# Last layer's product as seven block products over pairs of neighbouring token tiles

## The chip, the cores and the metric

The kernel runs on one core of a Trainium2 chip. The metric is the device time of one execution in microseconds (us). TensorE (PE) multiplies, VectorE (DVE), ScalarE (ACT) and GpSimd (POOL) work on vectors, and SyncE (SP) issues every transfer of this kernel. Each of the five runs its own list of instructions in order and waits for others on semaphores.

## The reference, cut to what matters

Two layers run over 2048 tokens (4 batches of 512) of 1024 features. What the change rewrites is the last step, the second layer's feed-forward part, and what it moves stands behind the product before it, the attention's output projection:

```python
out = einsum('bhqk,bkhd->bqhd', attn, v).reshape(B, S, H * VD)
return out @ wo.T                       # added to x by the caller

# _L1_ffn_ref, with x = layernorm of the stream
q = x[:, Q_START:Q_END, :].mean(axis=1)
routing = softmax(q @ router_W.T + router_b)
base = x @ W.T + b                      # W: 1024 x 1024
t = einsum('bsd,erd->bser', x, A)       # 8 experts x rank 16 = 128 columns
lora = einsum('bser,eor,be->bso', t, B, routing) * SCALING
return base + lora                      # added to x by the caller
```

## The kernel before, in words

Tokens stand in 16 tiles of 128, resident in SBUF as `xb` (128 partitions x 16 x 1024, f32). Every matrix product of f32 data is made of f16 halves: a value is scaled and split into a high f16 part and a low f16 part, and `mm3` (lines 46 to 50) issues three products, high by high, high by low and low by high, into the same accumulator bank. So three matmuls stand for one in all that follows.

**Making the halves.** `Norm` (line 57) gives mean and reciprocal deviation of a tile: DVE statistics (`dve_stats`, lines 83, 84, 87), POOL for the power (`pool_rstd`, lines 92, 95), DVE for the normed rows (`dve_apply`, line 105). `Feed` (line 113) then takes the high half on ACT (`act_high`, line 174), the low half on POOL (`pool_low`, line 179), and SP turns both by a transposing DMA (`sp_turn`, line 186), so that features stand on partitions.

**Output projection** (`out_projection`, line 2192; names `E_...`). For each of 16 tiles `j`, 16 blocks of `kt` are multiplied in two banks of 512 columns, 96 matmuls a tile. The attention's output stands in DRAM (`od`); SP turns tile `j` into one of three buffers `ow_ot` (`ow.sp_turn(e, j)`, line 668), which it may do once tile `j - 3` is multiplied (the wait on `s_col`). DVE adds each finished tile to `xb` (`add(j)`, line 2246). PE may start tile `j` when `ow_ot` has landed and `add(j - 3)` has freed the banks. Between those, SP loads the last layer's weights and squares for their scale are made on ACT (`lw.act_square`); the totals are made behind tile 9 (`TOTALS`), and after that weights are scaled and split (`lw.act_split` on ACT, line 1308, `lw.dve_split` on DVE, line 1315) straight into SBUF: four parts here, ten more at the start of the last function. The first three tiles' rows are normed behind tiles 3, 4 and 5 (`NORMED`).

**Last layer** (`lora_layer1`, line 2323; names `F_...`). The 1160 columns (8 of the router, 128 of the adapters' first factor, 1024 of the base matrix) are cut in three chunks of 392, 384 and 384 (`CH`). For each tile `columns(t, c)` runs 8 blocks of `k` by three matmuls into bank `F_o`, 24 matmuls a chunk, 72 a tile. ACT keeps the router's and the adapters' columns (`keep`, lines 2454, 2455); DVE adds the rest to the stream (`finish`, line 2534); POOL adds the bias (`add_bias`, line 2566). Once a batch of four tiles is through, the router's mean and softmax (`router`, line 2392 on PE), the turned and routed adapter rows (`turn_w`, line 2398; `high_w`, `low_w`, lines 2445 and 2512), and the adapters' second product (`adapter`, six matmuls of 512 columns into `F_tr`, read by line 2521) are set into the middle of later chunks by the list `inside`. For the last batch they stand in and behind the last chunks (`ORDER`). A finished tile goes out in one transfer (line 2584).

The order on each engine is written out by hand; nothing is scheduled by a program. Between two functions stands a barrier of all engines (the branch at line 2314).

Of the kernel before, what the change touches and what calls it, by code (L numbers as in the profile page):

```python
# [17 lines left out]
NT = 16  # L18
# [211 lines left out]
def layers(nc, a, out):  # L230
    root = ExitStack()
    with root:
# [25 lines left out]
        g["ow"] = ow = OutWeights(nc, root, mwd, od, ms)  # L258
        mid, banks = ExitStack(), ExitStack()
# [7 lines left out]
        with ExitStack() as right:  # L267
            with ExitStack() as both:
# [9 lines left out]
                first(**g)  # L278
# [3 lines left out]
                lora_layer0(**g)  # L282
# [7 lines left out]
        with ExitStack() as outs, ExitStack() as last:  # L290
            ow.place(outs)
            ow.ob = bk + [outs.enter_context(nc.psum_tensor("bk3", [128, 512], F))] + qu.qb
            attention(**g)
            mid.close()
            feed.place(last, "N1", "left", 2 * NT, (1, 2, 0))
            feed.hT = [keep[:, 1024 * i:1024 * i + 1024].bitcast(H16).rearrange("p (k c) -> p k c", k=2 * KD) for i in range(3)]
            lw.place(lambda name, shape, dt=F: last.enter_context(nc.sbuf_tensor(f"F1_{name}", shape, dt)), a,
                     [r[:, 0:784] for r in ow.raw])
            out_projection(**g)
            outs.close()  # L300
            banks.close()
            lora_layer1(**g)


class Scope:


    def __init__(self, nc, name):
        self.nc, self.name, self.ctx = nc, name, ExitStack()
# [8 lines left out]
    def sem(self, name):  # L318
        return self.ctx.enter_context(self.nc.semaphore(f"{self.name}_{name}"))
# [289 lines left out]
class OutWeights:  # L609
# [61 lines left out]
    def pe_turned(self, w, j, kt):  # L671
# [3 lines left out]
        else:  # L675
            w.wait_ge(self.s_o[j % 3], 16 * self.G * (1 if j % 3 else 2) + 16 * (j // 3))


def first(nc, a, wbd, mwd, cst, vec, half, ident, xb, norm, msq, lnr, room, feed, lw, ones, s_c, bk, keep, bias, s_xb, **_):
# [443 lines left out]
    ph.ctx.close()  # L1123


class Lora:
# [12 lines left out]
    def place0(self, sb, a, room):  # L1139


        self.L, self.a, self.ring, self.had, self.again = 0, a, 6, [0] * 6, 0
# [18 lines left out]
    def place(self, sb, a, raw):  # L1161


        self.L, self.a, self.raw = 1, a, raw
        self.sb = sb
        self.ring, self.had, self.again = 3, [3, 3, 2], self.N
        self.W = [self.pair("w", 0)]
        self.junk = sb("junk", [128, 784], H16)
        self.small()
        self.w_v = a["w1"].rearrange("(k p) n -> p k n", p=128)  # L1170

# [5 lines left out]
    def pair(self, what, c):  # L1177
        return [self.sb(f"{what}{c}{x}", [128, KD, CH[c][1]], H16) for x in "hl"]

    def place_rest(self, sb):  # L1180
        self.sb = sb
        self.W += [self.pair("w", 1), self.pair("w", 2)]
        self.BT = [sb("bh", [128, D], H16), sb("bl", [128, D], H16)]

    def split_done(self, w, n):

        w.wait_ge(self.s_wl, self.N * self.L + n + 1)
# [4 lines left out]
    def inverses_done(self, w, n):  # L1192

        w.wait_ge(self.s_inv, 2 * self.L + (1 if n < 5 else 2))

    def scale_done(self, w, c):

        w.wait_ge(self.s_sc, 3 if self.L else 2 if c else 1)

    def slot(self, q):  # L1200

        i = q % self.ring
        return i, self.had[i] + q // self.ring + 1
# [11 lines left out]
    def source(self, q):  # L1215

        c = self.PARTS[q % self.N][0]
        wd = CH[c][1] if c < 3 else 256
        return self.raw[q % len(self.raw)][:, 0:2 * wd].rearrange("p (k n) -> p k n", k=2)
# [7 lines left out]
    def sp_load(self, e, w, q):  # L1227
        c, k = self.PARTS[q % self.N]
        p = q - self.ring
        if 0 <= p < self.again or not self.L:  # L1230
            w.wait_ge(self.s_sq, self.N * self.L + p + 1)
        elif p >= 0:
            self.split_done(w, p - self.again)
# [3 lines left out]
        else:  # L1237
            e.dma_start(self.source(q), self.a[f"B{self.L}"][:, 512 * k:512 * k + 512].rearrange("p (k n) -> p k n", k=2)
                        ).then_inc(self.s_raw[self.slot(q)[0]], 16)

    def act_square(self, e, w, n):
        src = self.source(n)
        self.landed(w, n)
        w.wait_ge(self.s_sq, self.N * self.L + n)
# [3 lines left out]
    def pe_totals(self, e, w, ones, bank, n0=0, n1=N):  # L1248
        w.wait_ge(self.s_sq, self.N * self.L + n1)
# [23 lines left out]
    def dve_totals(self, e, w, bank, s_tot):  # L1273

        w.wait_ge(self.s_sum, 3)
# [1411 lines left out]
```

## Time and profile before

| What | Value |
|---|---|
| Median of 3 runs | 1598.59 us (1597.6 to 1601.69) |
| Profiled execution, first to last instruction | 1596.5 us |
| Median less that span | 2.1 us |
| PE busy | 1539.0 us, 96% |
| DVE, ACT, POOL busy | 1030.4, 878.4, 806.3 us |

Busy time says how long an engine had an instruction in it. For PE the length of one matmul row is not its cost, since matmuls overlap; the distance from one start to the next is. The function called output projection ends its products near 1373 us, the last layer's run from 1375 to 1592.6 us.

### The profile page before, as it was taken

Reading aid. Unit: us, or ns where it says so; the run is one execution under the profiler, and the core shown is the slowest. Engines: PE = TensorE matmul, PEld = TensorE weight load, DVE = VectorE, ACT = ScalarE, POOL = GpSimd, SP = SyncE. Lnnn points to the kernel's source line nnn. Section 1 sums busy time; section 2 is a strip of 40 time slices with the busy share of each in tenths; the row PEclk is TensorE's granted clock in tenths of the full one; section 3 lists DMA queues with packets and bytes.
Section 4 is the critical chain, followed back from the end, with each engine's and each line's share of the span. In section 5 each row is a group of like instructions: output and inputs, shape, how many; then the busy total and the mean of one; then the engine's idle time right before and its main releaser. Section 6 shows DMA issues by size and latency. Waiting matters only on the chain. (4 is left out here: it accounts for less than half of the span.)

```text
span 1596.5 us, 32012 instructions
## 1 busy us (share of the span) xinstructions
PE 1539.0 (96%) x12384; PEld 948.8 (59%) x12384; DVE 1030.4 (65%) x2745; ACT 878.4 (55%) x1665; POOL 806.3 (51%) x706
## 2 busy tenths in 40 slices
PE   5998999999999999999999999999999999999998
PEld 4656555555556777677777777644444444566564
DVE  8898869986778888888888888742110100444433
ACT  6887324323769999999999999941110000211110
POOL 4223244446948888888888888820100000244450
PEclk9999999999999999999999999999999999999999
DMA  9994245545939999999999999988763330223331
GB/s 366 317 327 149 67 94 145 159 132 127 165 83 165 190 179 180 189 189 198 186 199 186 194 177 188 187 214 221 192 150 79 80 93 1 87 62 80 93 80 66
DMA packets 556503, 248.78 MB, mean 156 GB/s; under 512 B 498368, under 2 KB 531264, under 8 KB 556224
## 3 DMA queue, kind: packets, MB, share of 16 engines
q1 hardware_dynamic: 556352, 246.74, 67.1%
q8 instruction: 98, 1.61, 0.4%
q14 instruction: 53, 0.43, 0.1%
HBM read 73.68 MB, written 48.23 MB: 76 GB/s over the span
## 5 line engine op out<-in xcount | busy, mean ns | idle before, releaser
L2128 POOL TENSOR_TENSOR xb<-xb 128x1280 f16<-128x1280 f32 x128 | 335.7, 2623 | 5.3 <-ACT xb L2031 5.3
L2023 ACT ACTIVATE xb<-bk,D_sv,qw_c 128x512 f32<-128x512 f32 (+3 forms) x512 | 289.1, 622 | 2.4 <-DVE D_sv L2086 2.2
L2077 DVE TENSOR_REDUCE bk<-bk 128x1 f32<-128x512 f32 (+3 forms) x512 | 227.8, 491 | 15.9 <-PE bk L1973 15.2
L2031 ACT ACTIVATE xb<-xb 128x1280 f16<-128x1280 f32 x128 | 162.7, 1271 | 12.2 <-DMA xb<-xb 8.5
L92 POOL TENSOR_SCALAR mv<-mv 128x1 f32<-128x1 f32 x64 | 27.6, 431 | 279.4 <-DVE mv L87 278.3
L1988 PE MATMUL D_t<-vh,xb 128*128 128x65 f16 x1280 | 130.8, 194 | 1.6 <-DVE D_on L2096 1.6
L1989 PE MATMUL D_t<-vl,xb 128*128 128x65 f16 x1280 | 130.9, 192 | 0.0
L1990 PE MATMUL D_t<-vh,xb 128*128 128x65 f16 x1280 | 130.3, 193 | 0.0
L2246 DVE SCALAR_TENSOR_TENSOR xb<-bk,ms_c,xb 128x512 f32<-128x512 f32 x22 | 15.5, 746 | 166.0 <-PE bk L50 166.0
L1988 PEld LDWEIGHTS D_t<-vh,xb 128*128 128x128 f16 x1280 | 118.7, 97 | 2.5 <-issue 2.2
L1989 PEld LDWEIGHTS D_t<-vl,xb 128*128 128x128 f16 x1280 | 118.4, 98 | 0.4
L1990 PEld LDWEIGHTS D_t<-vh,xb 128*128 128x128 f16 x1280 | 118.6, 97 | 0.0
L2566 POOL TENSOR_TENSOR xb<-xb,F_bias 128x1024 f32<-128x1024 f32 x16 | 38.2, 2394 | 131.7 <-DMA F_mean<-in_cst 131.7
L2134 POOL TENSOR_TENSOR D_os<-D_on,D_os 128x256 f16<-128x256 f32 x128 | 87.6, 685 | 6.8 <-ACT D_os L2046 6.8
L606 POOL TENSOR_TENSOR D_qs<-D_qs,keep 128x256 f32<-128x256 f32 x84 | 61.1, 727 | 56.3 <-DVE keep L601 56.3
L174 ACT ACTIVATE N_hl<-N_h 128x1024 f16<-128x1024 f32 x26 | 27.4, 1054 | 108.9 <-DVE N_h L105 108.7
L48 PE MATMUL bk<-E_mh,ow_ot 128*128 128x512 f16 x220 | 83.4, 379 | 0.0
L49 PE MATMUL bk<-E_ml,ow_ot 128*128 128x512 f16 x220 | 83.4, 379 | 0.0
L50 PE MATMUL bk<-E_mh,ow_ot 128*128 128x512 f16 x220 | 83.4, 379 | 0.0
L566 PE MATMUL bk<-kTh,keep 128*128 128x512 f16 (+3 forms) x256 | 76.7, 299 | 2.7 <-DVE keep L551 1.3
L566 PE MATMUL bk<-kTh,D_QTh 128*128 128x512 f16 (+3 forms) x256 | 76.7, 299 | 1.3 <-ACT xb L2023 1.2
L567 PE MATMUL bk<-kTl,D_QTh 128*128 128x512 f16 (+3 forms) x256 | 76.6, 299 | 0.0
(367 smaller groups left out, 4627.5 us busy)
## 6 DMA issues: line engine op xcount, KB each, us to landing
od<-D_os SPq DMA_DIRECT2D x32, 512.0 KB, 4.6
xd<-xb SPq DMA_DIRECT2D x16, 512.0 KB, 4.0
ow_raw<-mwd SPq DMA_DIRECT2D x32, 256.0 KB, 3.4
xb<-xd SPq DMA_DIRECT2D x16, 512.0 KB, 5.9
out_x<-xb SPq DMA_DIRECT2D x16, 512.0 KB, 2.9
xb<-in_x SPq DMA_DIRECT2D x6, 1024.0 KB, 14.3
A_wo<-in_wo SPq DMA_DIRECT2D x6, 1024.0 KB, 6.8
ow_raw<-in_w SPq DMA_DIRECT2D x16, 384.0 KB, 4.6
```

Source lines behind the costliest of these rows:

```text
L48: e.matmul(out, a[0], b[0], start=start, stop=False, **kw)
L49: e.matmul(out, a[0], b[1], start=False, stop=False, **kw)
L50: return e.matmul(out, a[1], b[0], start=False, stop=stop, **kw)
L566: e.matmul(ps, qh, kT[0][:, k0:k0 + M], start=i > 0, stop=False)
L1988: e.matmul(o, pt[:, c, :], v[0][:, t, 0:65], start=j == 0, stop=False)
L1989: e.matmul(o, pt[:, c, :], v[1][:, t, 0:65], start=False, stop=False)
L1990: m = e.matmul(o, pt[:, 10 + c, :], v[0][:, t, 0:65], start=False, stop=j == i)
L2023: m = e.activation(p[:, AT[i]:AT[i] + N], Sb[n % 4][:, c:c + N], ACT.Exp, scale=qw.col(qw.NEG, g), bias=s[:, 7 - i:8 - i])
L2031: e.activation(P2[u % 3][:, 0:1280], P[u % 3][:, :], ACT.Copy).then_inc(s_ph, 1)
L2077: m = e.tensor_reduce(minima(u, i), Sb[n % 4][:, c:c + N], AX.X, ALU.min)
L2128: e.tensor_tensor(P2[u % 3][:, 1280:2560], P[u % 3][:, :], P2[u % 3][:, 0:1280], ALU.subtract).then_inc(s_pl, 1)
L2134: e.tensor_tensor(o[:, :, 1, 64 * h:64 * h + 64], on[u % 2][:, :, :], o[:, :, 0, 64 * h:64 * h + 64], ALU.subtract).then_inc(s_ol, 1)
```

## The change

**In the last layer** tiles are taken in pairs, 2p and 2p + 1. With the two tiles as rows of blocks, the two halves of the 1024 features as columns of blocks, and the base matrix in four blocks of 512 x 512, the product of a pair is made of seven block products (4 blocks of `k`, 512 columns each) where the plain way has eight. For this `PairFeed` makes two more tiles of rows a pair, sums and differences of halves (`dve_sums`, four DVE instructions of 512), each of which is split and turned like a tile. Of the seven blocks of weights three are blocks of the base matrix and four (`T1` to `T4`) are sums of such blocks. The seven products go into four banks (`X` twice, `Y`, `Z`), some on top of others; DVE reads a bank after each product (`read`, seven reads of 512 columns a pair, the running sum of a bank being what is read), and later products into that bank wait for the read (`read_before`). The 136 columns of router and adapters are a product of their own (`gates`, 48 matmuls of 136 columns a pair), made between product 5 and 6 of the pair before. The adapters' work stands at fixed places in odd pairs (`ODD`), the router's in even ones (`EVEN`). The last tile's halves go out apart.

**In the output projection** the rows and sums of pair 0 are made on DVE behind `add(1)` instead of tiles 0 to 2 behind 3 to 5; totals stand behind tile 6 instead of 9. The weights are then prepared in eight pieces (four blocks of `k` by two halves of the columns): POOL makes four sums a piece (`pool_sums`), ACT and DVE split the seven blocks' pieces (768 and 1024 columns), into one single buffer `O` that lies in the free tiles 12 to 15 of `xb`, and SP stores them to DRAM (`w1d`, two transfers a piece). The table `LOWS` says behind which tile's `add` DVE does this: pieces 0 to 2 behind tile 7, 3 to 5 behind tile 8, 6 and 7 with router, adapters and `B` behind tile 9. SP stores them in the turn of the loop that follows. The blocks are loaded back: one in turn 11, three as the last tile frees the output projection's first weight buffers (`ow.early`), three at the start of the last layer.

**Elsewhere** `Scope` gives its semaphores back; POOL clears the first function's at the start of `lora_layer0`.

```diff
+    PREPARED = [(j, c) for j in range(4) for c in range(2)]
+    ITEMS = PREPARED + [("g", 0), ("g", 1), ("b", 0)]
...
+    def stored_before(self, n):
+        return 32 * min(n, 8)
+
+    def act_high(self, e, w, n):
+        w.wait_ge(self.s_sc, 1)
+        self.landed(w, n)
+        if n < 8:
+            w.wait_ge(self.s_sums, 4 * n + 4)
+        w.wait_ge(self.s_out, self.stored_before(n))
+        parts = self.splits(n)
+        for i, (o, src, kind) in enumerate(parts):
+            x = e.activation(o[0], src, ACT.Copy, scale=self.scale(kind))
+        x.then_inc(self.s_hi, 1)
+
+    def dve_low(self, e, w, n):
+        w.wait_ge(self.s_sc, 1)
+        w.wait_ge(self.s_hi, n + 1)
+        for o, src, kind in self.splits(n):
+            i = e.scalar_tensor_tensor(o[1], src, self.scale(kind), o[0], ALU.mult, ALU.subtract)
+        i.then_inc(self.s_lo, 1)
+
+    def sp_store(self, e, w, n):
+        x, c = self.ITEMS[n]
+        w.wait_ge(self.s_lo, n + 1)
+        for l in range(2):
...
+                to, of = self.w1d[:, :, l, x, 256 * c:256 * c + 256].rearrange("b p n -> p b n"), self.O[:, l, :, :]
+            e.dma_start(to, of).then_inc(self.s_out, 16)
...
 def out_projection(...)
-    NORMED, TOTALS = 3, 9
+    TOTALS = 6
+    LOWS = {7: (0, 1, 2), 8: (3, 4, 5), 9: (6, 7, 8, 9, 10)}
...
         for j in range(NT):
             add(j)
-            if NORMED <= j < NORMED + 3:
-                stats(j - NORMED)
-                feed.dve_apply(e, w, N1 + j - NORMED, xb[:, j - NORMED, :])
+            if j == 1:
+                for q in range(2):
+                    stats(q)
+                    pf.dve_apply(e, w, q, xb)
+                for part in range(2):
+                    pf.dve_sums(e, w, 0, part)
...
+            for n in LOWS.get(j, ()):
+                lx.dve_low(e, w, n)
...
         for j in range(G, NT):
             w.wait_ge(s_col, j - 2)
             ow.sp_turn(e, j)
...
+            for n in LOWS.get(j - 1, ()):
+                if n < 8 or n == 10:
+                    lx.sp_store(e, w, n)
+                if n + 3 < len(lx.ITEMS):
+                    lx.sp_load(e, w, n + 3)
...
 def lora_layer1(...)
+    PRODUCTS = [("X", 0, 0, lx.B11), ("Z", 0, 4, lx.B21), ("X", 2, 4, lx.T2), ("Y", 3, 0, lx.T3), ("X", 2, 0, lx.T1),
+                ("Y", 1, 4, lx.T4), ("X", 3, 4, lx.B22)]
+    EVEN = {11: "r"}
+    ODD = {0: "w0", 2: "a0", 3: "w1", 5: "a1", 6: "w2", 8: "a2", 9: "w3", 11: "a3"}
...
+    def read_before(p, i):
+        return [7 * (p - 2) + 7, 7 * (p - 1) + 2, 7 * p + 1, 7 * (p - 1) + 6, 7 * p + 3, 7 * p + 4, 7 * p + 5][i]
...
+        gates(0)
+        for p in range(NP):
+            for s in range(14):
+                half_product(p, s // 2, s % 2)
+                x = inside(p, s)
+                if x:
+                    {"r": router, "w": turn_w, "a": adapter}[x[0]](x[1])
+                if s == 9 and p + 1 < NP:
+                    gates(p + 1)
```

How the instructions move is shown at two places. The first is SP's list from tile 7's turn on in the output projection, before (`E_col` is the count of finished tiles, `W_sq` that of squares, `ow_ot` the turned tile, `keep<-N1_hl` a normed tile being turned):

```order
L668 DMA_TRANSPOSE ow_ot2<-od 128x32x128 [waits E_col]
L1236 DMA ow_raw0<-in_w1 128x2x392 [waits W_sq]
L1236 DMA ow_raw1<-in_w1 128x2x384 [waits W_sq]
L1236 DMA ow_raw2<-in_w1 128x2x384 [waits W_sq]
L668 DMA_TRANSPOSE ow_ot0<-od 128x32x128 [waits E_col]
L186 DMA_TRANSPOSE keep<-N1_hl0 128x16x128 [waits N_lo]
```

and in the changed kernel from tile 8's turn to tile 9's (the count of finished tiles is here printed `A_mst0`, since the semaphore is reused; `X_lo` counts the pieces whose low halves DVE has made):

```order
L679 DMA_TRANSPOSE ow_ot2<-od 128x32x128 [waits A_mst0]
L868 DMA w1d<-xb 128x7x256 [waits X_lo]
L868 DMA w1d<-xb 128x7x256
L811 DMA ow_raw2<-in_w1 128x2x256 x2
L868 DMA w1d<-xb 128x7x256 [waits X_lo]
L868 DMA w1d<-xb 128x7x256
L811 DMA ow_raw0<-in_w1 128x2x256 x2
L868 DMA w1d<-xb 128x7x256 [waits X_lo]
L868 DMA w1d<-xb 128x7x256
L811 DMA ow_raw1<-in_w1 128x2x256 x2
L679 DMA_TRANSPOSE ow_ot0<-od 128x32x128 [waits A_mst0]
```

Before, SP waits only for finished tiles and for squares; now three waits for DVE's pieces stand between the turn of tile 8 and the turn of tile 9, and the same again between 9 and 10, and between 10 and 11. The second place is DVE's list there in the changed kernel (line 2507 is `add`, line 857 a low half, `X_hi` the count of pieces whose high halves ACT has made):

```order
L2507 SCALAR_TENSOR_TENSOR xb<-bk2,ms_c,xb 128x512 [waits A_mst0]
L2507 SCALAR_TENSOR_TENSOR xb<-bk3,ms_c,xb 128x512
L857 SCALAR_TENSOR_TENSOR xb<-ow_raw2,F1_sc,xb 128x768 [waits X_hi]
L857 SCALAR_TENSOR_TENSOR xb<-xb,F1_sc 128x1024
L857 SCALAR_TENSOR_TENSOR xb<-ow_raw0,F1_sc,xb 128x768 [waits X_hi]
L857 SCALAR_TENSOR_TENSOR xb<-xb,F1_sc 128x1024
L857 SCALAR_TENSOR_TENSOR xb<-ow_raw1,F1_sc,xb 128x768 [waits X_hi]
L857 SCALAR_TENSOR_TENSOR xb<-xb,F1_sc 128x1024
L2507 SCALAR_TENSOR_TENSOR xb<-qb0,ms_c,xb 128x512 [waits A_mst0,A_wo1]
L2507 SCALAR_TENSOR_TENSOR xb<-qb1,ms_c,xb 128x512
```

The three pieces stand between `add(7)` and `add(8)`; before, nothing stood there.

## Rows read from the trace of the kernel before

**Rows 1.** The page: granted clock of PE in 40 slices, in tenths.

```profile
PEclk9999999999999999999999999999999999999999
```

**Rows 2.** Windows: output projection's middle and the last layer (stretch, length, busy by engine).

```profile
1207.00:1269.00 62.00, 62.00 (x290) 28.28 (x289) 4.93 (x11) 2.62 (x3) 1.02 (x1) 1.00 0.34 85
...
1400.00:1575.00 175.00, 175.00 (x1060) 104.29 (x1058) 68.72 (x137) 23.60 (x56) 71.53 (x48) 1.00 0.29 73
```

**Rows 3.** Timeline of PE (start, length) at 1206 us: first and last of 13 starts.

```profile
1205.67 0.38 PE L48 MATMUL bk<-E_mh,ow_ot 128*128 128x512 f16 x1
...
1208.26 0.38 PE L48 MATMUL qb<-ow_mh,ow_ot 128*128 128x512 f16 x1
```

**Rows 4.** The same at 1040 us: first and last of 30 starts; the page's weight loads.

```profile
1040.15 0.19 PE L1988 MATMUL D_t<-vh,xb 128*128 128x65 f16 x1 [1.65 <-DVE D_on L2096]
...
1041.04 0.19 PE L1990 MATMUL D_t<-vh,xb 128*128 128x65 f16 x1
...
L1988 PEld LDWEIGHTS D_t<-vh,xb 128*128 128x128 f16 x1280 | 118.7, 97 | 2.5 <-issue 2.2
```

**Rows 5.** Groups by shape, the last layer: one of three and one of six.

```profile
L50 PE MATMUL F_o<-F_w0h,keep 128*128 128x392 f16 x128 | 42.1, 329 | 0.0
...
L48 PE MATMUL F_o<-F_w2h,keep 128*128 128x384 f16 x128 | 41.7, 326 | 0.0
```

**Rows 6.** Turns of attention output from 1165 to 1210 us: SP's time, then landing.

```profile
L668 SPq DMA_TRANSPOSE ow_ot<-od x3: 4674/4703/5277, 1165.7 to 1207.2; - x3
...
DMA to landing us min/median/max: 6.7/6.7/8.9
```

**Rows 7.** Timeline of DVE: the additions of tiles 7 and 8.

```profile
1207.17 1.41 DVE L2246 SCALAR_TENSOR_TENSOR xb<-bk,ms_c,xb 128x512 f32<-128x512 f32 x2 [17.87 <-PE bk L50]
1227.96 1.41 DVE L2246 SCALAR_TENSOR_TENSOR xb<-qb,ms_c,xb 128x512 f32<-128x512 f32 x2 [19.38 <-PE qb L50]
```

**Rows 8.** High and low halves by ACT and DVE: 1024 columns, then 768 and 784.

```profile
L655 ACT ACTIVATE E_mh<-ow_raw,ms_c x10: 1147/1148/1149, 1060.5 to 1081.6; 128x1024 f16<-128x1024 f32 x10
...
L659 DVE SCALAR_TENSOR_TENSOR E_ml<-ow_raw,ms_c,E_mh x10: 1283/1284/1286, 1061.7 to 1082.8; 128x1024 f16<-128x1024 f32 x10
...
L1308 ACT ACTIVATE F_w2h<-ow_raw,F_sc 128x768 f16<-128x768 f32 x4 | 3.6, 931 | 3.0 <-DMA ow_raw<-in_w 3.0
...
L1315 DVE SCALAR_TENSOR_TENSOR F_w0l<-ow_raw,F_sc,F_w0h 128x784 f16<-128x784 f32 x3 | 2.9, 1026 | 0.0
```

**Rows 9.** Stores to DRAM: SP's time and landing, 510 to 700 us; the page's median.

```profile
L2160 SPq DMA_DIRECT2D od<-D_os x11: 431/575/643, 515.2 to 697.1; - x11
...
DMA to landing us min/median/max: 3.2/4.0/7.4
...
od<-D_os SPq DMA_DIRECT2D x32, 512.0 KB, 4.6
```

**Rows 10.** Windows of PE's one long pause and what followed.

```profile
136.00:137.00 1.00, 0.00 (x0) 0.00 (x0) 1.00 (x2) 1.00 (x3) 1.00 (x2) 1.00 0.00 0
...
138.00:139.00 1.00, 1.00 (x6) 0.49 (x4) 1.00 (x3) 0.42 (x2) 0.00 (x0) 0.50 0.46 168
...
141.00:142.00 1.00, 1.00 (x5) 0.88 (x5) 0.00 (x0) 1.00 (x4) 0.00 (x0) 0.95 0.24 92
```

**Rows 11.** Groups by shape, last layer: POOL; then DVE beside POOL's work.

```profile
L2566 POOL TENSOR_TENSOR xb<-xb,F_bias 128x1024 f32<-128x1024 f32 x16 | 38.2, 2394 | 131.7 <-DMA F_mean<-in_cst 131.7
L179 POOL TENSOR_TENSOR N_hl<-N_h,N_hl 128x1024 f16<-128x1024 f32 x13 | 28.4, 2184 | 13.4 <-ACT N_hl L174 13.4
...
L1315 DVE SCALAR_TENSOR_TENSOR F_w2l<-ow_raw,F_sc,F_w2h 128x768 f16<-128x768 f32 x4 | 7.0, 1794 | 3.1 <-ACT F_w2h L1308 3.1
```

**Rows 12.** The page: a normed tile being turned; then a POOL timeline row at 149 us.

```profile
keep<-N_hl SPq DMA_TRANSPOSE x16, 4.3
...
149.37 0.89 POOL L92 TENSOR_SCALAR mv<-mv 128x1 f32<-128x1 f32 x1 [9.16 <-DVE mv L87]
```

**Rows 13.** Timeline of DVE: the end.

```profile
1592.03 1.41 DVE L2521 SCALAR_TENSOR_TENSOR xb<-F_tr,F_sc,xb 128x512 f32<-128x512 f32 x2 [0.99 <-PE F_tr L50]
```

More of the change, by code:

```diff
@@ L294, in layers @@
             mid.close()
[L295 to L298, printed above, removed]
+            lx.place(lambda name, shape, dt=F: last.enter_context(nc.sbuf_tensor(f"F1_{name}", shape, dt)), ow, xb)
+            pf.place(lambda name, shape, dt=F: last.enter_context(nc.sbuf_tensor(f"P_{name}", shape, dt)), keep, xb)
             out_projection(**g)
@@ L1175, in small @@
         self.sc = self.sb("sc", [128, 20])
[L1177 to L1183, printed above, removed]
     def split_done(self, w, n):
-        w.wait_ge(self.s_wl, self.N * self.L + n + 1)
+        w.wait_ge(self.s_wl, n + 1)
     def all_split(self, w):
@@ L1303, in act_split @@
         c = self.PARTS[n][0]
-        self.landed(w, self.again + n)
+        self.landed(w, n)
         self.scale_done(w, c)
-        if c and not self.L:
+        if c:
             self.split_done(w, 4 * c - 1)
-        e.activation(self.halves(n)[0], self.source(self.again + n), ACT.Copy, scale=self.scale(c)).then_inc(self.s_wh, 1)
+        e.activation(self.halves(n)[0], self.source(n), ACT.Copy, scale=self.scale(c)).then_inc(self.s_wh, 1)
     def dve_split(self, e, w, n):
@@ L2426, in pe, with gates @@
-        for x in ORDER:
-            if x[0] == "c":
-                columns(x[1], x[2])
-            else:
-                small(x)
+        def gates(p):
+            for i in range(2):
+                hi, lo = pf.halves(4 * p + i)
+                pf.turned(w, 4 * p + i)
+                w.wait_ge(s_ta, 2 * p)
+                for k in range(KD):
+                    x = mm3(e, gb[:, GN * i:GN * i + GN], (hi[:, k, :], lo[:, k, :]), (lx.G[0][:, k, :], lx.G[1][:, k, :]),
+                            k == 0, k == KD - 1)
+                x.then_inc(s_g, 1)
@@ new lines, in half_product @@
+        def half_product(p, i, h):
+            _, kind, k0, blk = PRODUCTS[i]
+            hi, lo = pf.halves(4 * p + kind)
+            W = lx.pe_block(w, blk)
+            pf.turned(w, 4 * p + kind)
+            w.wait_ge(s_fin, read_before(p, i))
+            for k in range(2 * h, 2 * h + 2):
+                x = mm3(e, bank(p, i)[:, :], (hi[:, k0 + k, :], lo[:, k0 + k, :]), (W[0][:, k, :], W[1][:, k, :]),
+                        k == 0 and i in (0, 1, 3), k == 3, skip_group_check=i in (2, 4, 5, 6))
+            if h:
+                x.then_inc(s_p, 1)
@@ L2592, in sp, with store @@
-        for t in range(2, NT):
-            if t + 2 < NT:
-                feed.sp_turn(e, w, N1 + t + 2)
-            for c in range(3):
-                for y in inner(t, c):
-                    if y[0] == "a":
-                        store(y[1])
-        for t in (12, 14, 15):
-            store(t)
-        w.wait_ge(s_out, 16 * NT)
+        def store(q, halves=(0, 1)):
+            t = pf.tile(q)
+            for c in halves:
+                e.dma_start(out[128 * t:128 * t + 128, 512 * c:512 * c + 512], xb[:, t, 512 * c:512 * c + 512]).then_inc(s_out, 16)
```

661 lines of the change are left out of this document (414 added, 247 removed).

## The prediction, made before the changed kernel was run

> **What bounds the kernel now.** I read the page first, then the windows, the groups by shape and the timelines of the two stages that the change touches. The clock row shows PE at its upper level, 2.4 GHz, in all 40 slices [rows 1]. The windows show PE busy for 62.00 of 62 us in the middle of the output projection and 175.00 of 175 in the last layer, with DVE at 4.93 and 68.72 and POOL at 1.02 and 71.53 us there [rows 2]. So in both stages the end is set by how many columns PE streams, as long as nobody keeps it waiting; a column saved is time saved, and a wait added to PE is time added in full. The output projection gives one tile in 20.7 us (96 matmuls at the distance below; DVE's additions of tiles 7 and 8 start 20.79 us apart, [rows 7]).
>
> **What a matmul costs** is the distance between two starts. For 512 columns, 12 distances take 1208.26 - 1205.67 = 2.59 us, so 215.8 ns each, or 0.4215 ns a column [rows 3]. For 65 columns, 29 distances take 0.89 us, so 30.7 ns each, each with a weight load of its own [rows 4].
>
> **The last layer, PE.** Before: three groups of 128 matmuls of 392 columns and six of 384 [rows 5], so 16 x 24 x 1160 = 445,440 columns. After, a pair takes 7 products x 4 blocks x 3 = 84 matmuls of 512 columns and 48 of 136: 49,536 columns, in all 396,288. The difference is 49,152 columns x 0.4215 ns = **20.7 us less**. Adapters, turns and routers are the same instructions elsewhere in the order. A gate matmul is thereby priced at 136 x 0.4215 = 57 ns. The row of 65 columns lies at 30.7 ns, 3.3 above its columns, so a weight load does not bind at 57 [rows 4]. *The Trainium skill (TensorE: Matmul & The Clock Gate, Back-to-back issue gap) says that in a stream of load and matmul pairs N = 128 takes some 81 ns; by it 384 gate matmuls would cost 9 us more. The trace does not agree: the distance of the 65-column pairs is well under that.*
>
> **The last layer, waits.** DVE and POOL get more work. POOL has, a pair, four low halves, two biases and two powers: 4 x 2.18 + 2 x 2.39 [rows 11] + 2 x 1.3 (an estimate: 0.89 in [rows 12] and a power of about half a us behind it) = 16 us, against PE's 20.9 us in an even pair (49,536 columns) and 27 in an odd one (24 adapter matmuls x 0.2158 and four turns more). The chain norm, high, low, turn (4.3 us, [rows 12]), then the sum rows through the same two buffers, biases and powers comes to 21 or 22 us: it fits, with little over in even pairs. DVE's low halves took 1794 ns beside POOL's work where 784 columns alone took 1026 [rows 8, 11]; the new sums have, like those, two inputs in SBUF, so I take them at double, some 1.3 us each instead of 0.7. In odd pairs the statistics and a late adapter read stand before the bank that the fourth turn needs: about 1 us a pair, 4 us in all. At the start, bias transfer and first bias of POOL end about 9 us in while product 3 wants the first bank read at 8 us: 1.7 us. Sum of waits **+5.7 us**; bounds 1 us (DVE always in time) and 16 us (each even pair stretched by 4 us on top if the chain is 25 us). I take the first because the chain's rows fit.
>
> **The end.** Before, two adapter reads of DVE start at 1592.03 [rows 13], the second on the bank that PE ends last, and a transfer of 512 KB ends at 1596.5. After, one read follows the last product, and 256 KB go out. I put half of one read on it: **-0.4 us**.
>
> **The output projection.** PE's matmuls stay the same. What changes is who releases them. Call the time at which tile 7 is multiplied 0; the next tile ends at 20.7. DVE then adds tile 7 (1.4 us, [rows 7]) and makes three pieces. There is one buffer `O`: the high half of piece n + 1 waits until both transfers of piece n have landed. So the round trip is store, high, low, in series:
> - store: the second transfer is issued 0.57 us after the first and lands 4.6 us later [rows 9]: 5.2 us. A piece has 448 KB in each of its two transfers, in runs of 512 bytes; the row has 512 KB in one. Bounds: 0.4 + 3.2 = 3.6 and 0.6 + 7.4 = 8.0 us [rows 9].
> - high, 768 and 1024 columns on ACT: 0.93 + 1.15 = 2.1 us [rows 8].
> - low on DVE: 0.98 + 1.28 = 2.25 us (the row for 784 columns scaled) [rows 8].
>
> Round trip c = 9.5 us, between 7.9 and 12.3. The first piece's high half is ready in time (totals stand behind tile 6, a tile earlier), so the lows end at 3.65, 3.65 + c and 3.65 + 2c. Behind the third wait SP issues two stores and two loads (2 us) and only then turns tile 9, which lands 6.7 us later [rows 6]: 12.35 + 2c = 31.4 us. PE wants it at 20.7 us. **Wait at tile 9: 2c - 8.35 = 10.7 us.** This wait did not exist: before, the same turn was issued when tile 6 had ended, a whole tile and more ahead.
>
> The next three pieces follow the same beat, the turn of tile 10 lands at 12.35 + 5c; PE wants it at 33.05 + 2c. **Wait at tile 10: 3c - 20.7 = 7.8 us.** Pieces 6 and 7 end 2c later, the rest takes a store of 5.2 us and 3.8 us of halves (544, 544 and 1024 columns), issue and landing 7.5 us: the turn of tile 11 lands at 20.15 + 7c, PE wants it at 33.05 + 5c. **Wait at tile 11: 2c - 12.9 = 6.1 us.** Together 7c - 42 = **+24.6 us**, between 13 and 44. For turn 12 nothing is left to wait for, and DVE's delayed additions cost nothing, because PE needs `add(8)` only for tile 11.
>
> **The clock.** PE stood still for the whole of 136 to 137 us; at 138 to 139 the granted clock was 0.50, the 1.2 GHz level, and in 141 to 142 it was 0.95, back again [rows 10]. Some 3.4 us at half speed lose 1.7 us. The waits above are longer. Three times 1.7 is **+5.1 us**; bounds 0 and 8 (the longest wait followed by twice as much).
>
> **The rest.** The first rows are made from 1100 us on, when DVE has 16 us and more between tiles; squares and totals end before they are wanted; loads of the first four blocks have the last five tiles for themselves; the three at the start of the last layer (1 MB each) are wanted from 13 us on, and the first lands about 8 us in. All at 0; if a block came late it would be by 1 to 2 us. POOL's clearing of 38 semaphores falls in a stretch in which it then waited 9.16 us for DVE [rows 12]: 0, at most 1 us.
>
> **Sum**: 24.6 + 5.1 - 20.7 + 5.7 - 0.4 = **+14.3 us**. The profiled execution of 1596.5 us and 2.1 us around it are just the median of 1598.6 us, so the forecast is **1612.9 us**. A measurement of this kernel can tell about 0.3%, 4.8 us, from no change: faster is below 1593.8, slower above 1603.4.
>
> **Rivals.**
> - *The round trip is short and the saved columns win.* Place: the store between two highs. With c = 7.9 the waits are 13.3 us, the last wait in the clock is small, say two drops, 3.4; with waits of 3 us in the last layer: 13.3 + 3.4 - 20.7 + 3 - 0.4 = -1.4, 1597 us, no change. To be faster c must be under 7.3 us, which needs a store of 2.9 us, below the shortest of [rows 9], unless stores are quicker here than in those rows, which stand beside the attention's own transfers. At c = 6.8: 5.4 for tile 9, then nearly nothing for 10, and 1 for 11: 6.4 + 2 - 20.7 + 3 - 0.4 = -9.7, **1589 us**. Against it: ACT and DVE alone take 4.35 of it. Chance of c that short 0.11, of the middle 0.13.
> - *The last layer is bound by its feed.* DVE's sums and POOL hold each other up, and the chain of an even pair takes 25 us instead of 21 or 22: four even pairs, some 10 us more, **1623 us**. For it: the 1794 ns of [rows 11]; against it: POOL's 16 us of work. Chance 0.12.
> - *Gate matmuls are bound by loading weights.* A load row is 97 ns long [rows 4]; if 384 gates took that instead of 57, 15 us more, **1628 us**; by the page's 81 ns it would be 9 us more. The 30.7 ns speak against it. Chance 0.03.
> - *The waits are there, but the change of products is not what saves*: if the seven products' bank order stalls PE at each product by the read (0.7 us and 0.3 us of delay against a product of 2.6 us), 56 x 0.3 = 17 us more. Each read has a whole product's time, so chance 0.01.
>
> **How the numbers follow.** The forecast, slower by 5 to 25 us, gets 0.60. Faster: 0.11 of the first rival and a little for errors that I don't see, 0.13. No change: 0.13, and the lower edge of the forecast, 0.02, is 0.15. Slower: 0.72. The range leaves out the fastest and the slowest tenth: from 1594 (c of 7.5) to 1630 (c of 11, or the feed on top).
>
> **What would show it.** Tile 9, 10 and 11 of the output projection start 11, 8 and 6 us late, each released by a turn (DMA on `ow_ot`), and the clock falls behind them. SP's longest waits are on DVE's low halves; ACT's highs wait for the stores (`w1d`). From store to the next high 5 us. The last layer's PE time is 197 us of work in a stretch of about 203. If PE has no pause at tile 9, the account of the output projection is wrong; if the last layer takes over 207 us, that of its feed is.

## The result, and the profile after

| | before | after |
|---|---|---|
| median of the runs, us | 1598.09 (1595.74 to 1601.69, 4 runs) | 1614.72 (1612.97 to 1617.57, 4 runs) |
| ratio to before, 95% interval | | 1.0104 (1.0087 to 1.0121) |
| profiled span, us | 1596.5 | 1614.9 |
| add of tile 7 to add of tile 15 | 165.9 us | 192.4 us |
| add of tile 15 to the end | 223.4 us | 212.3 us |

The change makes the kernel 1.0% slower: 1614.7 us against a forecast of 1612.9 us. The last layer became 11.1 us shorter, and the output projection in front of it 26.5 us longer. Of the 18.4 us between the two profiled spans, 3.0 lie ahead of tile 7's add (1210.18 against 1207.17 us). The nine kernels of the experiments run the changed kernel's code up to there and make this add at 1206.2 to 1209.7 us, so most of the 3.0 is the spread of single executions; the medians differ by 16.6. One of the four executions of the first experiment's kernel took 4651 us, with its granted clock at 1.00 and for a reason that nothing here shows; its median of 1591.01 us includes it, and the other three have a median of 1589.54.

The page of the changed kernel, with PE's share and the clock that answers to [rows 1]:

```profile
PE 1527.1 (95%) x12288; PEld 925.7 (57%) x12288; DVE 1095.9 (68%) x2791; ACT 899.0 (56%) x1680; POOL 858.8 (53%) x754
...
PEclk9999999999999999999999999999998999999999
```

One slice of the clock row, at three quarters of the span, now reads 8. All of PE's waits from 1085 us to the end (line, what it waited for: us in total, times, longest):

```profile
PE bk L48 <- DMA ow_ot<-od: 17.5, 2, 12.9
PE F_tr L2674 <- DVE xb L2788: 5.5, 9, 0.9
PE qb L48 <- DMA ow_ot<-od: 3.9, 1, 3.9
PE F_X L48 <- DVE xb L2799: 3.1, 4, 2.4
PE F_g L48 <- DMA F_hT<-P_hl: 2.3, 2, 1.8
PE F_g L48 <- PEq L2595: 1.8, 1, 1.8
```

Three waits for turns of the attention output come first, 21.4 us together. Where [rows 2] showed PE busy for 62.00 of 62 us, these are the first matmuls of tiles 9, 10 and 11 in PE's timeline (start, length, and in brackets the wait and its releaser):

```profile
1243.79 0.59 PE L48 MATMUL bk<-ow_mh,ow_ot 128*128 128x512 f16 x1 [12.93 <-DMA ow_ot<-od]
...
1271.75 0.58 PE L48 MATMUL bk<-ow_mh,ow_ot 128*128 128x512 f16 x1 [4.55 <-DMA ow_ot<-od]
...
1298.76 0.38 PE L48 MATMUL qb<-ow_mh,ow_ot 128*128 128x512 f16 x1 [3.93 <-DMA ow_ot<-od]
```

Why each turn is late stands in SP's timeline of the same stretch (start, time on the queue, transfer, count). Two stores, two loads, and only then the turn:

```profile
1232.53 0.97 SPq L868 DMA_DIRECT2D w1d<-xb  x2
1233.54 2.40 SPq L811 DMA_DIRECT2D ow_raw<-in_w  x2
1235.98 5.68 SPq L679 DMA_TRANSPOSE ow_ot<-od  x1
```

From the turn's issue to PE's start it is 1243.79 - 1235.98 = 7.8 us. What SP waits for is DVE's low half of a piece, and these follow at a steady beat. The low halves in DVE's timeline; ACT's high half releases them:

```profile
1211.50 1.01 DVE L857 SCALAR_TENSOR_TENSOR xb<-ow_raw,F_sc,xb 128x768 f16<-128x768 f32 x1
...
1220.92 1.02 DVE L857 SCALAR_TENSOR_TENSOR xb<-ow_raw,F_sc,xb 128x768 f16<-128x768 f32 x1 [7.21 <-ACT xb L850]
...
1230.28 1.02 DVE L857 SCALAR_TENSOR_TENSOR xb<-ow_raw,F_sc,xb 128x768 f16<-128x768 f32 x1 [7.15 <-ACT xb L850]
```

The beat is 9.4 us; the first and the sixth piece start 1258.41 - 1211.50 = 46.9 us apart, 9.38 each. And the clock, in windows of PE (stretch, length, busy PE, PEld, DVE, ACT, POOL, granted clock, DMA share, GB/s):

```profile
1234.00:1242.00 8.00, 0.00 (x0) 0.00 (x0) 2.21 (x2) 1.97 (x2) 1.45 (x3) 0.58 1.05 257
1242.00:1246.00 4.00, 2.21 (x6) 0.87 (x7) 0.00 (x0) 0.00 (x0) 2.81 (x4) 0.50 1.08 280
...
1270.00:1274.00 4.00, 2.25 (x6) 0.87 (x7) 0.77 (x1) 0.00 (x0) 0.00 (x0) 0.50 0.87 226
```

PE came out of its 12.93 us wait at the 1.2 GHz level, and from its first matmul to its add tile 9 took 1267.24 - 1243.79 = 23.4 us instead of 20.7.

That slow tile reaches the chain of pieces at one place. In DVE's list piece 6 stands behind tile 9's add, and the add waited for PE:

```profile
1267.24 1.41 DVE L2507 SCALAR_TENSOR_TENSOR xb<-bk,ms_c,xb 128x512 f32<-128x512 f32 x2 [6.62 <-PE bk L50]
1268.56 1.01 DVE L857 SCALAR_TENSOR_TENSOR xb<-ow_raw,F_sc,xb 128x768 f16<-128x768 f32 x1
```

The sixth low half had begun at 1258.41, so this one comes 10.2 us behind it instead of 9.4.

In the last layer, the new sums of DVE (groups by shape from 1402 us on: busy us, mean ns):

```profile
L935 DVE TENSOR_TENSOR ow_raw<-ow_raw 128x512 f32<-128x512 f32 x7 | 13.9, 1986 | 0.0
L936 DVE TENSOR_TENSOR F_s<-ow_raw 128x512 f32<-128x512 f32 x7 | 12.5, 1782 | 0.0
L941 DVE TENSOR_TENSOR F_s<-ow_raw 128x512 f32<-128x512 f32 x7 | 10.3, 1466 | 0.2
L939 DVE TENSOR_TENSOR ow_raw<-ow_raw 128x512 f32<-128x512 f32 x7 | 6.0, 859 | 0.0
```

The gate matmuls went as the columns say, not as their weight loads do. The first and third in PE's timeline:

```profile
1404.29 0.22 PE L48 MATMUL F_g<-F_gh,keep 128*128 128x136 f16 x1 [1.77 <-PEq L2595]
...
1404.41 0.22 PE L50 MATMUL F_g<-F_gh,keep 128*128 128x136 f16 x1
```

Two distances are 0.12 us: 60 ns each for 136 columns, where 57 had been put down.

### The profile page after: what moved, and what is told of

Read it like the earlier page. It is cut to its first block and busy times, and to the rows that moved or that the text cites. A ratio compares the mean times of both kernels' runs of the same rounds, so it can differ in the third digit from the quotient of the medians.

```text
span 1614.9 us, 32082 instructions
## 1 busy us (share of the span) xinstructions
PE 1527.1 (95%) x12288; PEld 925.7 (57%) x12288; DVE 1095.9 (68%) x2791; ACT 899.0 (56%) x1680; POOL 858.8 (53%) x754
## 5 line engine op out<-in xcount | busy, mean ns | idle before, releaser
L92 POOL TENSOR_SCALAR mv<-mv 128x1 f32<-128x1 f32 x64 | 22.1, 346 | 147.5 <-DVE mv L87 146.5
L2739 ACT ACTIVATE F_lg<-F_g,F_sc 128x8 f32<-128x8 f32 x16 | 4.3, 269 | 133.3 <-PE F_g L50 133.3
```

## The experiments

Theory A: the loss is SP's order. The turns of tiles 9 to 12 stand in one queue behind stores that wait for a 9.4 us round trip. The saving is real, and part of it is lost again in the last layer to sums of DVE. Rivals: the turns are late because DMA is busy, wherever they stand; the clock's fall is a cost of its own; each of the three waits is a fixed price; the last layer's waits follow from DVE's amount of work.

**The turns ahead of the stores.** The turns of tiles 9, 10 and 11 are issued ahead of the stores of pieces 0, 3 and 6, in place of behind the whole group of stores that such a piece begins, and tile 12's ahead of the last store (item 10, `B`).

```diff
+        AHEAD = {0: 9, 3: 10, 6: 11, 8: 12}
...
         for j in range(G, NT):
-            w.wait_ge(s_col, j - 2)
-            ow.sp_turn(e, j)
+            if j not in AHEAD.values():
+                turn(j)
...
+                if n in AHEAD:
+                    turn(AHEAD[n])
```

> SP's list alone is changed: the turn of tiles 9, 10, 11 and 12 is issued ahead of the stores of pieces 0, 3, 6 and 10, as soon as its own condition holds (tile j - 3 multiplied). DVE's, ACT's and POOL's lists and the single buffer O stay. Theory A (the cost in the output projection is the queue position of the turns behind the round trips of O): PE waits for no turn, the clock does not fall there, the round trip stays 9.4 us. Output projection 21.4 + 5.1 = 26.5 us shorter, total about 1588 us, some 10 us below the kernel before. Rival B (the added transfers themselves slow the turns, or DVE's low halves delay the additions that PE needs): the waits move to the additions or the turns still land late; total stays above 1605 us.

Measured: 1591.01 us, ratio 0.9945 (0.9925 to 0.9964) to the kernel before. PE's waits for turns are down from 21.4 to 0.5 us:

```profile
PE qb L48 <- DMA ow_ot<-od: 0.5, 1, 0.5
```

Tile 7 to tile 15 is 166.4 us, as before the change. The whole loss of the output projection hangs on these few places in SP's list; the same transfers still ran beside it. With its turns there the change makes the kernel 0.55% faster. The same kernel was run again:

> The kernel with the four turns ahead of the stores once more, as the base of this batch: 1591.0, within 1.5 us, ratio 0.9945 to the kernel before; last layer 213 us.

Measured: 1590.29 us, ratio 0.9947 (0.9934 to 0.996); add of tile 15 to the end 212.1 us.

**Only the turn of tile 9 ahead** (`AHEAD = {0: 9}`).

> Only the turn of tile 9 goes ahead of the stores. Theory A: the round trips go on at their own beat and the turns of tiles 10 and 11 are still behind them, so the wait at tile 9 vanishes and nearly all of it comes back at tile 10: 12.35 + 5c against 41.4 us with c = 9.4 gives 18 us there instead of 4.6, then 4 to 6 us at tile 11. Total within 4 us of the changed kernel, about 1612 us. Rival C (each block of three pieces costs its own wait, independent of the others): 12.9 us and one fall of the clock, 2.7 us, are saved, total about 1599 us.

Measured: 1612.84 us, ratio 1.0086 (1.0069 to 1.0103). The wait at tile 9 is gone and stands at tile 10:

```profile
PE bk L48 <- DMA ow_ot<-od: 20.1, 1, 20.1
...
PE qb L48 <- DMA ow_ot<-od: 0.7, 1, 0.7
```

So the three waits are not three prices. The time at which a turn behind the stores can land is set by the number of pieces ahead of it, and PE waits for it in one part or in three.

**The pauses filled.** PE runs 56, 20 and 16 matmuls into the bank `tot`, whose contents nobody reads again, ahead of tiles 9, 10 and 11, to stand still less: 4.4 us of waits for turns are left of 21.4. They are added work; nothing is left out.

```diff
+        FILL = {9: 56, 10: 20, 11: 16}
...
+            if j in FILL:
+                w.wait_ge(lx.s_inv, 2)
+                for n in range(FILL[j]):
+                    e.matmul(tot[:, :], ow.m(0, 15)[:, 0:128], ow.m(0, 15)[:, 0:512], start=True, stop=True)
```

> The changed kernel, with 56, 20 and 16 matmuls of 512 columns on data of no use issued ahead of tiles 9, 10 and 11, which end about when the turns land (12.1, 4.3 and 3.5 us of work against waits of 12.9, 4.6 and 3.9); they write a bank that nobody reads after. If the clock is what makes tiles 9 and 10 take 23.4 and 23.1 us instead of 20.7 (theory A), it stays at 2.4 GHz and the total is 5 us less, about 1610 us. If those tiles are slow for another reason (stores, loads and PE's reads in each other's way, rival D), they stay at 23 us and the total does not fall, 1615 us or a little more.

Measured: 1615.04 us, ratio 1.0097 (1.008 to 1.0114). At tile 9 the clock stayed up:

```profile
1234.00:1242.00 8.00, 6.55 (x32) 2.78 (x30) 2.21 (x2) 1.97 (x2) 2.81 (x4) 1.00 1.09 261
1242.00:1246.00 4.00, 4.00 (x20) 1.83 (x19) 0.10 (x1) 1.97 (x2) 0.00 (x0) 1.00 0.72 206
```

At tile 10 it did not. After a wait of 2.96 us PE came back at the upper level and fell to the lower one 1.1 us later (two of its rows at 1269.7 and 1270.2 us, matmuls 0.22 and then 0.43 us apart):

```profile
1269.71 0.38 PE L49 MATMUL bk<-ow_ml,ow_ot 128*128 128x512 f16 x1
...
1270.21 0.63 PE L48 MATMUL bk<-ow_mh,ow_ot 128*128 128x512 f16 x1
```

Tile 9 took 20.9 us instead of 23.4, tile 10 22.6 instead of 23.1. So PE's tiles got 3.0 us shorter, and hardly anything of it arrived: from tile 7's add to tile 11's start it is 88.2 us against 88.6, and tile 7 to tile 15 is 192.0 us against 192.4. Part of that is the fill's own doing: the turn of tile 11 landed at 1293.9 (issued at 1286.96, 6.9 us to landing), and PE was still filling until tile 11 began at 1294.70. Without this 0.8 us some 1.2 of the 3.0 us would have arrived. The expected gain of 5 us was a miss, and it shows the flaw in my account of the clock. The next turn lands when SP's beat lets it; a slow tile mostly uses up the wait that comes after it.

**The beat shortened.** On the changed kernel, turns behind the stores as in it: each piece's high half is stored as soon as ACT has made it, and only the low half waits for DVE.

```diff
-        w.wait_ge(self.s_lo, n + 1)
         for l in range(2):
+            w.wait_ge(self.s_hi if l == 0 else self.s_lo, n + 1)
```

> Base: the changed kernel itself, turns behind the stores as in it. Each piece's high half is stored as soon as ScalarE has made it, not when VectorE has made the low half as well, so that the round trip (beat c of the pieces, 9.4 us in the changed kernel) gets shorter. Theory A (the waits at tiles 9 to 11 add up to 7 beats less a fixed 42 us): c falls by about 0.9 us (VectorE's low half of 0.9 us and one issue of 0.5 us come off, if the second store's landing doesn't take their place), the wait of ow_ot from 21.4 us to about 15 us, T7 to T15 from 192.4 to about 186 us, total about 1608. If the second store's landing ends the beat as before: c falls by 0 to 0.5 us, total 1611 to 1615. Rival B (the three waits are each a turn's own landing, whatever the beat): waits and total as in the changed kernel, 1614.7, also with a shorter beat.

Measured: 1608.10 us, ratio 1.0062 (1.005 to 1.0074), 6.6 us under the changed kernel. The beat between low halves that follow each other without a turn fell to 7.6 us:

```profile
1209.57 1.01 DVE L857 SCALAR_TENSOR_TENSOR xb<-ow_raw,F_sc,xb 128x768 f16<-128x768 f32 x1
...
1217.12 1.02 DVE L857 SCALAR_TENSOR_TENSOR xb<-ow_raw,F_sc,xb 128x768 f16<-128x768 f32 x1 [5.34 <-ACT xb L850]
...
1232.29 1.02 DVE L857 SCALAR_TENSOR_TENSOR xb<-ow_raw,F_sc,xb 128x768 f16<-128x768 f32 x1 [1.85 <-ACT xb L850]
1241.81 1.02 DVE L857 SCALAR_TENSOR_TENSOR xb<-ow_raw,F_sc,xb 128x768 f16<-128x768 f32 x1 [7.31 <-ACT xb L850]
```

That is 1.8 us shorter, twice what I had expected, but the beat across a turn is 9.5 us (the last two rows): the next high half's store now comes while SP is still busy with the turn. From the first low half to the eighth it is 58.2 us where it was 68.0, so 8.3 us a beat. PE's waits for turns fell from 21.4 to 13.5 us, and tile 7 to tile 15 from 192.4 to 183.6 us. A shorter beat shortens the total, as the formula of the prediction has it: with c = 8.31 it gives 16.2 us, and tile 11 starts 77.4 us after tile 7's add against 62.1 before, 15.3 us late. Three fixed prices would have left it.

**The sums copied.** On the kernel with the turns ahead: the sums of pairs 1 to 7 are replaced by copies with one input, of the same size and at the same place. Left out are these sums.

```diff
-        if part == 0:
+        if p and part == 0:
...
+            e.tensor_scalar(sa[:, lo], h2[:, lo], 1.0, None, ALU.mult).then_inc(self.s_sum, 1)
+            e.tensor_scalar(sb[:, lo], h1[:, lo], 1.0, None, ALU.mult).then_inc(self.s_sum, 1)
...
```

> On top of e1_turn_first. In pairs 1 to 7 the four sums of rows a pair are replaced by plain scaled copies of one input, so the output leaves out the sums; number, width and place of the instructions are the same, but each reads one SBUF operand instead of two. Theory E (DVE's two-input sums are held up by POOL's instructions, 2 to 2.6 us instead of 0.7, and that makes bank reads and adapter reads late): the copies take 0.4 to 0.7 us each, PE's waits in the last layer fall from about 10 us to 4 or less, total about 6 us below e1_turn_first. Rival F (the waits come from the places of the adapters' work in the order, and would be there with any DVE work in between): the waits stay near 9 us and the total within 2 us of e1_turn_first.

Measured: 1586.82 us, ratio 0.9921 (0.9905 to 0.9938), last layer 207.7 us, 5.5 less than its base in the same batch. But the copies were held up too, if less (the page's groups, busy us and mean ns):

```profile
L935 DVE TENSOR_SCALAR ow_raw<-ow_raw 128x512 f32<-128x512 f32 x7 | 12.1, 1722 | 0.0
L936 DVE TENSOR_SCALAR F_s<-ow_raw 128x512 f32<-128x512 f32 x7 | 10.6, 1518 | 0.0
L939 DVE TENSOR_SCALAR F_s<-ow_raw 128x512 f32<-128x512 f32 x7 | 8.7, 1245 | 0.0
L938 DVE TENSOR_SCALAR ow_raw<-ow_raw 128x512 f32<-128x512 f32 x7 | 4.2, 595 | 0.0
```

I had expected 0.4 to 0.7 us each, which one of the four keeps to. PE's listed waits in the last layer fell from 11.9 us to 9.1, not to 4: those on DVE from 8.6 to 4.2, while the one on `F_hT` grew from 1.5 to 3.1. So the last layer does hang on how long DVE's four instructions take, some 0.25 us a sum here, but one input in place of two is no way out.

**The sums elsewhere.** The same sums, later in DVE's list: in steps 2 and 5 of pairs 1, 3 and 5, behind the reads that free PE's banks, and in steps 5 and 7 of pair 0; in pairs 2, 4 and 6 they keep their places. The statistics of odd pairs move from step 7 to step 9 with them.

```diff
+        SUMS_AT = [(5, 7)] + [(2, 5) if p % 2 else (1, 3) for p in range(1, NP)]
...
-                if p + 1 < NP and s in (1, 3):
-                    pf.dve_sums(e, w, p + 1, s // 2)
-                if p + 2 < NP and s == 7:
+                if p + 1 < NP and s in SUMS_AT[p]:
+                    pf.dve_sums(e, w, p + 1, SUMS_AT[p].index(s))
+                if p + 2 < NP and s == (9 if p % 2 else 7):
```

> Base: the kernel with the four turns ahead of the stores. Only the places of VectorE's sums move: for a pair that follows an odd pair they come after the adapter's product has been read and after the next pair's product (steps 2 and 5 in place of 1 and 3), the first pair's at steps 5 and 7. Theory A (the waits of F_tr and F_X in the last layer are there because a sum of VectorE, held up beside POOL by up to 2 us, stands ahead of the subtraction that frees the product's bank): those two waits fall from 8.6 us to about 3 us together, last layer about 208.5 us from the add of tile 15 to the end in place of 213.2, total 4 to 5 us below the base, about 1586.5. Rival B (VectorE is late by its whole amount of work, wherever the sums stand): the waits only move to other products, total within 1.5 us of the base, about 1591.

Measured: 1582.63 us, ratio 0.9905 (0.9892 to 0.9918), 7.7 us under its base in the same batch. The waits of `F_tr` and `F_X` on DVE fell from 8.7 to 0.7 us:

```profile
PE F_g L48 <- DMA F_hT<-P_hl: 4.0, 2, 3.6
PE F_g L48 <- PEq L2603: 1.8, 1, 1.8
...
PE F_X L48 <- DVE xb L2807: 0.7, 3, 0.2
```

The sums that moved also came to lie where POOL stands idle. DVE in pair 3, in the kernel with the turns ahead, with POOL's low half (line 962) that the first sum runs into (line 2796 is the read of the adapters' bank `F_tr`):

```profile
1461.23 2.13 POOL L962 TENSOR_TENSOR P_hl<-ow_raw,P_hl 128x1024 f16<-128x1024 f32 x1 [3.75 <-ACT P_hl L957]
...
1461.87 2.03 DVE L935 TENSOR_TENSOR ow_raw<-ow_raw 128x512 f32<-128x512 f32 x1
...
1464.43 1.40 DVE L2796 SCALAR_TENSOR_TENSOR xb<-F_tr,F_sc,xb 128x512 f32<-128x512 f32 x2
...
1467.57 2.50 DVE L941 TENSOR_TENSOR F_s<-ow_raw 128x512 f32<-128x512 f32 x1
```

and in this one:

```profile
1462.05 1.41 DVE L2796 SCALAR_TENSOR_TENSOR xb<-F_tr,F_sc,xb 128x512 f32<-128x512 f32 x2 [1.19 <-PE F_tr L50]
1463.37 0.68 DVE L935 TENSOR_TENSOR ow_raw<-ow_raw 128x512 f32<-128x512 f32 x1
...
1469.52 0.69 DVE L941 TENSOR_TENSOR F_s<-ow_raw 128x512 f32<-128x512 f32 x1
```

So the sums now stand behind the read of `F_tr`, and they are no longer held up: two of four took 2.03 and 2.50 us beside POOL, and all four take 0.68 or 0.69 with POOL idle. Over pairs 1 to 7 DVE's sums fell from 42.7 to 30.1 us in all. The run can't say which of the two took PE's waits away, and with less work of DVE it doesn't refute rival B cleanly either. The pairs that kept their places show that long sums alone need not cost much: their first two still take 1.99 and 2.61 us, and PE waits 0.24 us for `F_X` there, before and after. Add of tile 15 to the end is 205.4 us. What is left is new: the second pair's gates wait 3.6 us for the turn of their rows.

**The start of the last layer, ACT and POOL.** Rows 4 and 5 made ahead of other work there.

```diff
+        pf.act_high(e, w, 4)
         keep(0)
         keep(1)
...
+        pf.pool_low(e, w, 4)
         add_bias(0)
+        pf.pool_low(e, w, 5)
         add_bias(1)
...
```

> Base: the kernel with the sums later. At the last layer's start the high and the low half of row 4 and POOL's first halves are made ahead of the copies for the gates' second turn. Theory A (the gates of the second pair wait 1.5 to 3 us for their rows' second turn because of what stands ahead of it on ScalarE and POOL): these waits on F_hT and the one on the sequencer fall from 3.3 us to below 1.5 us, total 1 to 2 us below the base, about 1585. Rival B (the wait is for keep, which now comes later): the wait moves there and the total is the base's or up to 1 us above, 1587.

Measured: 1582.10 us, ratio 0.9898 (0.9885 to 0.9911), which can't be told from its base. The wait stayed at 4.1 us, so it was not what stands ahead of it on ACT and POOL. SP's timeline showed where it came from: row 4's low half was made at 1380.3, its turn issued behind the last of ten loads,

```profile
1376.07 0.33 SPq L2863 DMA_DIRECT2D F_bias<-in_b  x1
...
1380.06 0.57 SPq L877 DMA_DIRECT2D F_w3h<-w1d  x1
...
1384.90 0.48 SPq L2869 DMA_DIRECT2D F_bl<-b1d  x1
1385.43 19.61 SPq L966 DMA_TRANSPOSE F_hT<-P_hl  x4
```

and the gates were released at 1395.8, 10.4 us after that.

**The start of the last layer, SP.** The turns of rows 4 and 5 between the loads of the weights, which are wanted later.

```diff
         pf.sp_turn(e, w, 3)
-        for i in range(4, 7):
-            lx.sp_load_block(e, w, i)
+        lx.sp_load_block(e, w, 4)
+        pf.sp_turn(e, w, 4)
+        lx.sp_load_block(e, w, 5)
+        pf.sp_turn(e, w, 5)
+        lx.sp_load_block(e, w, 6)
...
```

> Base: the kernel with the last layer's start reordered on ScalarE and POOL. On SyncE the turns of rows 4 and 5 now stand behind two and four of the ten loads at the last layer's start in place of behind all ten (9 weight and constant loads, 3.75 MB after F_bias; row 4's turn was issued 5.1 us after its low half was made and landed 10.4 us after its issue, as did the loads around it after 7 to 9 us). Theory A (the gates of the second pair wait for turns that are queued behind these loads): the waits of F_g on F_hT fall from 4.1 us to below 1 us, total 3 to 4 us below the base, 1578 to 1579. Rival B (the turns' chain itself, two buffers and some 9 us each, sets it): row 6 and 7's turns are as late as before, the waits fall by less than 1 us, total 1581 to 1582. Rival C (the weights come too late now): new waits on F_w6h or F_w2h.

Measured: **1577.73 us, ratio 0.9869 (0.9852 to 0.9885)**, 4.4 us under its base by the medians of two batches, and the fastest of all: 1.3% faster than the kernel before, 37 us faster than the changed one. PE's waits from 1085 us to the end:

```profile
PE F_g L48 <- PEq L2603: 1.8, 1, 1.8
PE F_X L48 <- DVE xb L2808: 1.5, 4, 0.8
PE F_tr L2676 <- DMA F_mean<-in_cst: 0.9, 1, 0.9
```

The waits on `F_hT` are gone; in their place a constant that is now loaded late costs 0.9 us. Add of tile 15 to the end is 201.8 us.

## Why the prediction was right, and where its sum was not

The sign, the places and the mechanism of the loss (turns behind round trips) and of the saving (columns) were right. The clock's part in it was not, and the waits in the last layer were put too low; the sum was within 2 us because these two errors cancel, and that is luck.

- **The columns, -20.7 us: confirmed.** The last kernel's layer takes 201.8 us against 223.4, with the same 4.2 us of PE's waits in it as before the change, and PE's busy time in it is 194.53 us against 215.35: 20.8 us less. The gates' distance was 60 ns where 57 had been put down; the rival that weight loads bind them (97 ns, or the 81 ns of the Trainium skill's page TensorE: Matmul & The Clock Gate, section Back-to-back issue gap) is refuted by it.
- **The round trip, c = 9.5 us: 9.4 measured.** The rival with a short trip fell. Its size was not far off, though: storing the high half at once gave 7.6 us between neighbours and 8.3 over seven beats.
- **The waits at tiles 9 to 11, 7c - 42 = 24.6 us: total right, parts not.** From tile 7's add to tile 11's start the changed kernel took 88.6 us against 62.1, so 26.5 more: 21.4 us of waits and 5.1 us of slow tiles inside them. With c = 9.38 the formula gives 23.7. At tile 9 it gives 10.4 us where 12.93 were measured, because two loads hold SP for 2.4 us, not the 0.9 that I took, and the turn needed 7.8 us to PE's start, not 6.7. The total misses something else: pieces 6 and 7 came 10.2 and 10.9 us behind the one before and not 9.4, 2.3 us together. Piece 6 stood behind tile 9's add; piece 7's high half began 6.7 us after piece 6's stores were issued, where it is 5.2 for the first piece. The second and third wait were predicted at 7.8 and 6.1 and were 4.55 and 3.93.
- **The clock, +5.1 us: the step that failed.** It was added on top of waits that had been reckoned as if PE ran at full speed. PE did lose 2.7 us at tile 9 and 2.4 at tile 10 at the lower level, but the landing of the next turn hangs on SP's beat, so most of it was given back in the next wait. The run with filled pauses shows it: tiles 9 and 10 took 3.0 us less and tile 11 started 0.4 us earlier (1.2 without the fill's own overrun). What did come through is the 0.8 us or so by which tile 9's late add held up piece 6. Only a fall behind the last wait costs something: in the changed kernel there was none (tile 11's first matmul has its usual 0.38 us), in the kernel with the shorter beat there was one, and from tile 11's start to tile 15's add it took 106.2 us instead of 103.8.
- **The waits in the last layer, +5.7 us: some 10 measured** (20.7 of columns and 0.7 of the end, less the 11.1 gained; PE's rows show 12.7 us against 4.2 before, and the remaining 1.8 lies in no wait that is listed). By the sign that the prediction gave itself, a last layer of over 207 us, its account of the feed was wrong: from PE's first start to its last end it is 207.4 us (1404.29 to 1611.66), where about 203 had been forecast. The start was put at 1.7 for POOL's first bias and is 2.4, a wait of `F_X`: DVE's first read did wait 4.7 us for that bias, but PE's wait went when the sums moved, with the bias where it was; the four odd pairs were put at 1 each, and the nine waits of `F_tr` are 5.5. I took DVE's sums at 1.3 us beside POOL; they took 1.99, 1.78, 1.47 and 0.86. With POOL idle such a sum takes 0.69 us; beside POOL it is up to 1.9 us longer, where a whole low half of POOL takes 2.1 to 2.5 us. The Trainium skill (SBUF — State Buffer, Who interferes with whom) says that the port pair which DVE and POOL share is an exclusive lock, and that a DVE instruction with two SBUF inputs contends for it with a POOL instruction that reads SBUF; the 2.03 and 2.50 us beside POOL agree. My doubling of the time was too little for the longest and too much for the others. Of POOL's 16 us of work in a pair the prediction was right that it doesn't bind: other places for the sums in DVE's list took 7.7 us off, by their order, by the hold-up that they avoid, or by both. The 1.8 us on PE's sequencer at the layer's start stands in every one of these kernels.
- **The start.** The loads at the layer's start were put at 0 because they are wanted later. That was true of the loads, not of the turns behind them: 2.3 us of the changed kernel's waits, and 4 us once the rest was out of the way.

In the sum: output projection +26.5 (29.7 predicted), last layer -11.1 (-15.4 predicted), so 15.4 against 14.3. The end took 0.7 us less than before (from PE's last start to the end of the span 3.6 us against 4.3), where 0.4 was put down.

What stays open: why a pair of loads holds SP for 2.4 us in the changed kernel and 1.6 with the high halves stored first; whether the order of the sums or their hold-up beside POOL made PE wait; and where the 1.8 us of the last layer are that no listed wait has (PE's busy time in it is 196.44 us in the changed kernel and 194.53 in the last one, with the same 1200 rows).

## What to carry to other kernels

When work moves into a stage that PE fills completely, read every queue that it passes through: the saving was real, but the turns of three tiles stood in SP's list behind a wait that had nothing to do with them, and moving them and a fourth by a few lines was worth 24 us. A wait in a serial chain should be counted against the clock of the chain, not of the engine: what the engine loses between two such waits comes back in the next, as long as no step of the chain waits for the engine (here one did, and let about 0.8 us through). And an experiment that removes one cause shows the next: other places for the sums and for the turns behind the loads were worth 12 us more, and neither was large enough to see while the first stood.

## What the runs showed of the hardware that was not expected

- Copies with one input in SBUF (f32, 512 columns, TENSOR_SCALAR) are held up beside POOL almost like sums with two: 1722 and 1518 ns in the mean against 1986 and 1782, where each takes 0.41 and 0.68 us with POOL idle. The same section of the Trainium skill counts such copies, in a mode that uses both port pairs, among the instructions that contend; the trace agrees.
- A turn issued behind 3.75 MB of loads on the same queue is released late: 10.4 us from issue to the gates' start, where the turns of [rows 6] landed 6.7 us after issue. The loads themselves took longer to land the further back they stood, 4.6 us for the first behind the turn before and 9.0 for the last; with turns between them none took more than 6.3 us.
- Pauses of almost the same length did not leave the same clock. In the changed kernel PE came out of 12.93 and 4.55 us at the lower level, its last slow matmul starting 4.6 and 4.2 us after the first, and out of 3.93 us at the upper one; in the kernel with the shorter beat it came out of 4.04 us at the lower one, its last slow matmul starting 4.6 us after the first; and in the kernel with filled pauses it came out of 2.96 us at the upper one and fell to the lower 1.1 us later.
